# First-layer attention: contraction rows widened to 97 and 128, zero rows and limit rows loaded by DMA

## The reference

```python
q = (latent @ Wq_up).reshape(Bsz, Tlen, N_HEAD, HEAD_DIM)
kv = latent @ Wkv_up
k, v = (kv[..., :HEAD_DIM], kv[..., HEAD_DIM:])
scale = 1.0 / np.sqrt(HEAD_DIM)
att = jnp.einsum('bthd,bsd->bhts', q, k) * scale
causal = jnp.tril(jnp.ones((Tlen, Tlen), dtype=bool))
att = jnp.where(causal[None, None], att, -jnp.inf)
att = jax.nn.softmax(att, axis=-1)
y = jnp.einsum('bhts,bsd->bthd', att, v).reshape(Bsz, Tlen, C)
```

## Time and profile before

| | us |
|---|---|
| median of 3 runs | 948.38 |
| lowest, highest | 939.05, 956.61 |
| the profiled execution | 954.41 |
| its span, first to last instruction | 952.7 |
| mean granted TensorE clock of the span | 0.875 of 2.4 GHz |

### The profile page before, as it was taken

The page is one execution under the profiler, slowest core; times in us unless marked ns, Lnnn a source line. Parts: engine busy times, 40 slices in busy tenths (PEclk is TensorE's granted clock), DMA queues, the critical chain, the costliest instruction groups (busy, mean ns, idle before and its releaser), DMA issues.

```text
span 952.7 us, 22934 instructions
## 1 busy us (share of the span) xinstructions
PE 801.5 (84%) x9158; PEld 405.7 (43%) x9158; DVE 553.2 (58%) x1503; ACT 449.8 (47%) x726; POOL 399.6 (42%) x531
## 2 busy tenths in 40 slices
PE   4577988898989899988688999988985778999887
PEld 3223333334343334424334444443433445666555
DVE  2574656656666565715577533330248758888875
ACT  1003545435454455655232433333324858888663
POOL 5101012323232230321000688878755569886423
PEclk9656979869797788989599998887995989999999
DMA  5730343244344123122300133333330011111111
GB/s 138 132 71 9 89 131 86 52 97 139 95 79 97 47 71 90 44 56 74 115 0 1 48 43 45 45 43 44 33 44 23 6 26 26 24 35 24 24 28 34
DMA packets 73838, 54.98 MB, mean 58 GB/s; under 512 B 23677, under 2 KB 66734, under 8 KB 73134
## 3 DMA queue, kind: packets, MB, share of 16 engines
q1 hardware_dynamic: 63878, 45.96, 19.8%
q0 software_dynamic: 9856, 7.58, 6.1%
HBM read 31.76 MB, written 18.23 MB: 52 GB/s over the span
## 4 chain that ended last, share of the span: by engine, by line
PE 49%; DVE 15%; POOL 12%; DMA 9%; issue 7%; ACT 3%; SPq 3%; POOLq 1%; DVEq 0%; ACTq 0%
POOL d_acc L1354 7%; PE bank L458 7%; PE ps_s L421 7%; PE bank L437 7%; DVE MX L854 3%; PE b1ps L2048 3%; PE ps_s L417 3%; DMA Q<-d_m 3%; PE b1ps L2059 3%; POOL XG L1344 3%; DMA d_m<-ms 2%; PE ps_o L1558 2%; PE b1ps L2072 2%; PE ps_h L1546 2%; DVE R L1450 1%
## 5 line engine op out<-in xcount | busy, mean ns | idle before, releaser
L854 DVE TENSOR_REDUCE MX<-bank 128x1 f32<-128x320 f32 (+13 forms) x352 | 185.7, 565 | 120.3 <-PE bank L465 119.4
L639 ACT ACTIVATE PR<-ps_s 128x1024 f32<-128x1024 f32 x160 | 160.4, 1023 | 169.5 <-PE ps_s L417 98.3
L458 PE MATMUL bank<-K,Q 72*32 72x32 bf16 (+15 forms) x2048 | 128.7, 330 | 31.7 <-DMA Q<-d_q 15.3
L421 PE MATMUL ps_s<-Q,K 75*32 75x512 bf16 (+1 forms) x1088 | 118.1, 423 | 16.2 <-DMA Q<-d_m 16.1
L458 PEld LDWEIGHTS bank<-K,Q 72*32 72x32 bf16 x2048 | 51.3, 109 | 113.4 <-issue 34.1
L437 PE MATMUL bank<-PR,VE 128*32 128x512 f32 x640 | 97.9, 693 | 0.0
L1354 POOL DMA_INDIRECT d_acc<-Y,idx x56 | 87.6, 1565 | 20.4 <-issue 16.5
L1558 PE MATMUL ps_o<-H,w 128*128 128x512 f32 x176 | 89.6, 660 | 0.0
L1344 POOL DMA_INDIRECT XG<-d_tab,idx x56 | 53.8, 961 | 78.6 <-DVE idx L1459 62.1
L1678 ACT ACTIVATE H<-ps_h,b1T 128x512 f32<-128x512 f32 x88 | 60.4, 687 | 42.3 <-PE ps_h L1546 39.9
L465 PE MATMUL bank<-maskQ,identb 128*32 128x32 bf16 (+3 forms) x1408 | 74.6, 207 | 0.0
(11 more groups left out here) (344 smaller groups left out, 1403.3 us busy)
## 6 DMA issues: line engine op xcount, KB each, us to landing
Q<-d_q SPq DMA_DIRECT2D x24, 384.0 KB
d_q<-qs SPq DMA_DIRECT2D x24, 128.0 KB, 2.4
X<-L_attn_x SPq DMA_DIRECT2D x8, 256.0 KB, 4.9
w<-L_ffn_W SPq DMA_DIRECT2D x8, 256.0 KB, 4.0
d_acc<-zrow SPq DMA_DIRECT2D x1, 2048.0 KB, 9.5
w<-L_ffn_W SPq DMA_DIRECT2D x1, 2048.0 KB, 9.6
AC<-d_acc SPq DMA_DIRECT2D x8, 256.0 KB, 2.9
d_y<-ysb SPq DMA_DIRECT2D x112, 18.0 KB
```

The lines of the kernel that those rows point to most:

```text
L421: last = nc.tensor.matmul(out_, k_[0:r, P * i + o:P * i + o + QW], q_[0:r, :, P * g + QW * j:P * g + QW * j + QW], start=True, stop=True, ...
L458: nc.tensor.matmul(mx[o:o + QW, x * w:(x + 1) * w], Q[b % QB][0:NPR, 4 * c + hh, QW * j:QW * j + QW], K[b % QB][0:NPR, 0:w], start=(x == 0 ...
L639: nc.scalar.activation(by_head.rearrange("p h (c x) -> p c h x", x=QW), ps_s[half][:, :].rearrange("p (c h x) -> p c h x", c=2, x=QW), ACT ...
L854: nc.vector.tensor_reduce(MX[b % 2][:, c:c + len(cs)], ring[R0.place["max", G]][:, 0:len(cs) * w].rearrange("p (x w) -> p x w", w=w), AX_X ...
```

## The change

The contraction of the products goes from 72 or 75 rows to `KF` = 97, that of the tiles on the limit and of the fills to 128. The limit pattern moves to rows 97 to 127, rows 75 to 96 are zero in `Q` (in row 96 `K` holds the first of the limit values), and `KC` and `QC` grow to 56 and 53 rows. Since the maxima now contract rows 72 to 74 too, where `K` is -1, these rows of `Q` must be zero until the maxima are known: one more DMA per batch writes them, ahead of the loads of `Q`. The limit rows of the three buffers are written at three places, with a semaphore each, and the maxima of batches 0 to 2 wait for them in place of the first scores.

```diff
-KQ = KM + QW
+KF = P - QW + 1
...
+LIMIT_ROWS = [(-2, 1), (-2, 7), (-1, 2)]
+QIN = 16 * (2 * PARTS + 1)
...
-    KC = sb0("KC", [PARTS + QW, T], BF16)
-    QC = sb0("QC", [QW, T], BF16)
+    KC = sb0("KC", [P - NPR, T], BF16)
+    QC = sb0("QC", [P - KM, T], BF16)
...
                     if i == g and kt > j:
-                        last = nc.tensor.matmul(out_, maskT[0:1, QW:2 * QW], bc(identb[0:1, 0:1], [1, 512]),
+                        last = nc.tensor.matmul(out_, maskT[:, QW:2 * QW], bc(identb[:, 0:1], [P, 512]),
                                                 start=True, stop=True, tile_position=(0, o))
                     else:
-                        r = KQ if i == g and kt == j else KM
+                        r = P if i == g and kt == j else KF
...
-                    pe.wait_ge(DS[f"q_in{b % 2}"], 96 * (b // 2 + 1))
+                    pe.wait_ge(DS[f"q_in{b % 2}"], QIN * (b // 2 + 1))
+                    if b < QB:
+                        pe.wait_ge(s_kc[b], 32)
...
-                                         Q[b % QB][0:NPR, 4 * c + hh, QW * j:QW * j + QW],
-                                         K[b % QB][0:NPR, 0:w], start=(x == 0), stop=False, tile_position=(0, o),
+                                         Q[b % QB][0:KF, 4 * c + hh, QW * j:QW * j + QW],
+                                         K[b % QB][0:KF, 0:w], start=(x == 0), stop=False, tile_position=(0, o),
...
-                if n == -1 and s == 0:
+                if (n, s) in LIMIT_ROWS:
+                    i = LIMIT_ROWS.index((n, s))
                     sp.wait_ge(s_eye, 1)
-                    for i in range(QB):
-                        sp.dma_start(K[i][NPR:KQ, :], KC[:, :]).then_inc(s_kc, 16)
-                        sp.dma_start(Q[i][KM:KQ, :, :], bc(QC[:, :].unsqueeze(1), [QW, NH, T])).then_inc(s_kc, 16)
+                    sp.dma_start(K[i][NPR:P, :], KC[:, :]).then_inc(s_kc[i], 16)
+                    sp.dma_start(Q[i][KM:P, :, :], bc(QC[:, :].unsqueeze(1), [P - KM, NH, T])).then_inc(s_kc[i], 16)
...
                     sp.wait_ge(DS[f"q_st{par}"], 48 * (b // 2 + 1))
+                    sp.dma_start(Q[b % QB][NPR:KM, :, :], bc(QC[0:PARTS, :].unsqueeze(1), [PARTS, NH, T])
+                                 ).then_inc(DS[f"q_in{par}"], 16)
```

More of the change, by code:

```diff
@@ L304, in program @@
     s_mq = sem("block_mask_ready")
-    s_kc = sem("limit_rows_loaded")
+    s_kc = [sem(f"limit_rows_loaded{i}") for i in range(QB)]
     s_lw = sem("late_weights_loaded")
@@ L403, in scores_T @@
                 pe.wait_ge(s_modR, 2)
-                pe.wait_ge(s_kc, 32 * QB)
             if s == 0 and half == 0:
@@ L941, in gpsimd_part @@
                                    in_=KC[:, :].rearrange("r (a x) -> r a x", x=QW), compare_op=ALU.not_equal, fill=-BIG,
-                                   base=-PARTS, pattern=[[0, NQB], [-1, QW]], channel_multiplier=1))
+                                   base=NPR + 1 - KF, pattern=[[0, NQB], [-1, QW]], channel_multiplier=1))
         lk(nc.gpsimd.memset(KC[0:PARTS, :], -1.0))
@@ L946, in gpsimd_part @@
                                    in_=QC[:, :].rearrange("r (a x) -> r a x", x=QW), compare_op=ALU.is_ge, fill=0.0,
-                                   base=-1, pattern=[[0, NQB], [-1, QW]], channel_multiplier=1))
+                                   base=KM - KF, pattern=[[0, NQB], [-1, QW]], channel_multiplier=1))
         nc.gpsimd.drain().then_inc(s_eye, 1)
@@ L1108, in sync_part @@
                     if b >= 2:
-                        sp.wait_ge(DS[f"q_in{par}"], 96 * (b // 2))
+                        sp.wait_ge(DS[f"q_in{par}"], QIN * (b // 2))
                     for i in range(NT):
```

## The result

| | before | after |
|---|---|---|
| median of the runs, us | 950.75 (4 runs) | 1011.59 (4 runs) |
| lowest, highest | 939.05, 956.61 | 1009.51, 1014.68 |
| profiled execution's span | 952.7 | 1007.7 |
| first score of the attention | 79.0 | 167.7 |
| attention, first score to last | 365.6 | 331.9 |

The changed kernel takes 1.0686 times as long, with a 95% interval of 1.0578 to 1.0795. Ratios and intervals go by the fast executions of each kernel alone and medians by all, which is why this one lies above 1.064, the ratio of the medians. I had predicted 900.

The account below looks back on a forecast made before the run. TensorE was taken as the bound, stretched by time at 1.2 GHz and by fills not overlapping products. 31.5 + 25 - 7 - 1 = 48.5 us took the profiled 954.4 to 906, and the median to 900; range 875 to 932.

Parts of the forecast that it names:

- Term 1: Diagonal steps: 128-row fills start with their products, gaining 1.26 us a step, 40.3 us over 32 steps.
- Rival C: Diagonal steps: fills still run apart, because of their constant operand and not their row count; 943 us, chance 0.08.
- Term 2: Diagonal step 9, during the maxima's chain: its gain becomes a longer wait; 8.8 us lost, 31.5 left.
- Term 3: TensorE's clock in the attention: less time at 1.2 GHz, gaining 25 us; bounds 0 and 52.
- Term 4: Attention periods: TensorE waits more often for VectorE's reductions, 1 us a period, 7 us lost.
- Term 5: TensorE's products: columns set the time, so 97 and 128 contraction rows cost nothing; bounds -1 and +1.
- Term 6: SyncE's queue: start stays, give or take 2 us; with the DMA of zeros 1 us lost, bounds -3 and +15.
- Rival B: Attention: the clock does not answer and VectorE takes a share of the gain; 932 us, chance 0.12.
- A: Attention: the clock comes back wholly, gaining 52 us there and not 25; 873 us, chance 0.13.
- D: SyncE's queue: added DMAs make Q late, 77 us lost less 48.5 gained; about 977 us, chance 0.05.

Follow-up runs that it names:

- fills_64: Kernel before, with the fills contracting 64 rows instead of 1; 950.7 us in one run, kernel before beside it 949.3.
- fills_65: Kernel before, with the fills contracting 65 rows instead of 1; 922.6 us in one run, kernel before beside it 949.3.
- fills_only: Kernel before, with only the six fills of a diagonal step contracting 128 rows instead of 1; median 921.7 us, 0.9685 of before.
- limit_53_only: Kernel before, with its three Q limit-row DMAs at their old place but 53 rows each instead of 32; 1040.4 us in one run.
- rows_48_5: Changed kernel, with each Q limit-row DMA of 53 rows written as two, 5 and 48 rows; median 933.6 us, 0.983 of before.
- scores_97_old_place: maxima_72 with all limit rows back behind batch 0's Q loads and the scores waiting for them; median 904.8 us, kernel before beside it 942.6.
- maxima_72: rows_48_5 with the maxima contracting 72 rows again and no DMA of zeros; median 919.6 us, 0.966 of before.
- rows_97_fills_1: rows_48_5 with the fills contracting one row again; median 967.5 us, 1.013 of before.
- zeros_early: rows_48_5 with the DMA of zeros moved ahead of the store of q; median 924.8 us, 0.972 of before.
- fills_only_again: fills_only unchanged, run again on the same chip as scores_97_old_place; median 911.4 us, kernel before beside it 942.6.

## Why the prediction was wrong, point by point

*Term 1, the fills.* Right in mechanism, and in size as an upper bound. I had 1.26 us a diagonal step, 0.84 of it in the first half; the timeline after shows 0.45 for 1.27 us in step 0, 0.61 in step 2, and in step 5 nothing is left of it behind the wait for VectorE. That it is the row count, and from 65 rows on, fills_64 and fills_65 show. Rival C falls.

*Term 2, what is hidden.* Right where it could show. I had 8.8 us of gain turn into waits for the maxima's chain; fills_only has 10.2 us more of them (26.3 - 16.1). In the changed kernel it is 3.7 us more, beside the longer waits for Q.

*Term 3, the clock.* Right in sign and size: 25 us were forecast, that is 50 us less at 1.2 GHz. Before it is 104 us, in the changed kernel 53 (a clock of 0.92 over 331.9 us). That it came out so near is in part luck: I had taken the term near the middle of wide bounds. Fills alone bring it to 64. Whether rows of zeros count had been left open; see below.

*Term 4, VectorE.* Near in size, wrong in what is waited for. TensorE's waits for reductions (`MX` at L461), from 20 to 520 us, are 3.8 us in all after, from 2.7, where I had 7 us more. The wait for VectorE that grew is the one in step 5, for `VE`, from 0.9 to 5.0, so that it is 5.2 us in all. Rival B falls: the clock did answer.

*Term 5, contraction rows.* Right: 512 columns take 0.38 to 0.39 us with 97 and with 128 rows.

*Term 6, SyncE's queue and the start.* This is the step that failed, twice. I wrote "So the start stays where it is, give or take 2 us", and it moved by 88.7. I had counted rows and bytes (106 against 96 rows) and never asked how one DMA is dealt out among the 16 engines. 32 rows became 53, and with that the DMA moved at the pace of a single engine: 36 us for each, and behind it a queue that cannot issue. limit_53_only and rows_48_5 show it from both sides. The Trainium skill states how a DMA is dealt out, in DMA: Bandwidth & Descriptors, section Why a DMA increments its semaphore by 16 and not by 1: the number of engines is the largest one up to 16 that divides the slowest dimension of both access patterns. By it 32 and 48 rows go over 16 engines, 53, a prime, over 1, and the DMA share of 0.07 agrees. With 24 GB/s for one engine, the row count alone gives the three times 36 us. Without them the start would have stayed nearly where it was: the first score is at 79.0 before, at 77.2 with all limit rows at their old place (scores_97_old_place), at 80.2 with buffer 0's at the early one (maxima_72) and at 83.6 with the zeros as well (rows_48_5).

Second, "I take 1 us" for the zeros. They cost some 14 us (rows_48_5 against maxima_72). I had set the issue at 0.35 us; it is 0.76 us and 1.3 us more for the next DMA, and Q lands later on top. And I had said that it "is needed some steps later only". That was true of the kernel before, with 3.8 us of waits for Q within its attention. It is not the shorter periods that made it false: fills_only, with an attention of 321.9 us, has 2.1 us of them, while rows_97_fills_1, with the zeros and one-row fills, has 18.6 in an attention of 362.5. By the rule of the same page of the Trainium skill a DMA of three rows runs on three engines; that this is why the next one is held up was not tried apart.

*The rivals.* A falls: the clock was back in part only. D, at 0.05, had the right family (added DMAs make Q late), but the wrong place and price: it laid 70 of its 77 us on the later batches and 7 on the start, and the start took 88.7.

*The sum.* (ScalarE's seven periods add up to 169.7 us and not 169.8; nothing hangs on it.) Without term 6 the forecast of 900 stood on a gain of 49.5 us. fills_only gained 29 in the median and scores_97_old_place 38, so that even where the DMAs do no harm the sum was some 12 to 21 us too high. Up to the end of the attention it was not: in the profiles the last score comes at 444.6 us before, at 400.4 in fills_only and at 394.1 in scores_97_old_place, 44.2 and 50.5 us earlier. For fills_only the missing part lies outside what I summed: the work behind the attention is the same in all kernels, took 508.1 us before and after, and 504.5 to 520.8 in the experiments' profiles (fills_only: 918.0 - 400.4 = 517.6; scores_97_old_place: 898.6 - 394.1 = 504.5). The profiles fall into two groups. In the seven where this part took 516.7 to 520.8 us (rows_48_5, fills_only, rows_97_fills_1, limit_53_only, maxima_72, fills_64, fills_65), TensorE has a single wait of 7.5 to 11.2 us at the experts' first matmuls (`ps_h`); in the five where it took 504.5 to 509.5 none there is over 2.2. So some 10 us between two totals can come from a part that no edit touched, and differences of that size are better read at the end of the attention. What brings this wait about was not tried and stays open.

## What to carry to other kernels

Before you change the shape of a DMA, look at the count in its outermost dimension and not at its bytes: split 53 rows into 48 and 5, and 84 of the 89 us lost at the start are back. In a trace a DMA share of about 1/16 beside an issue row of tens of us, behind a harmless looking DMA, is the mark of one. And matmuls of 1 and of 64 rows did not run beside those of 75 and 107 rows; giving them idle rows cost nothing here and gained the 29 us of fills_only.

## What the runs showed of the hardware that I had not expected

- A queue is held up by one busy engine although 15 are idle: DMAs of 6 to 56 KB behind a DMA at one engine's pace (24 GB/s) were not issued for 28 to 40 us (changed kernel, limit_53_only).
- A 48 KB DMA of three rows makes the issue of the next ones 1.3 us longer, for both kinds seen (loads of Q 2.43 for 1.13 us in rows_48_5, store of q 3.24 for 1.88 in zeros_early).
- The step between 64 and 65 contraction rows of a fill beside products of 75 and 107: 0.32 against 0.21 us from start to start.
- Rows that hold only zeros may go with less time at 1.2 GHz. With fills that overlap, the kernels with 72 and 75 rows had 58 to 72 us of it in the attention (fills_only 64, fills_65 58, fills_only_again 72), those with 97 rows 38 to 53; each figure is good to some 3 us, since the clock is read to two digits. Once the DMAs that come with it were out of the way, the pair on one chip was 6.5 us apart. With one-row fills it is 102 us before, 86 in limit_53_only and 73 in rows_97_fills_1. These are single profiles: limit_53_only has the very attention of the kernel before and yet 16 us less, and fills_64, with 72 and 75 rows and gaps, had 56 us. That the rows are the cause is made likely by the pair on one chip, not shown.
